# Loading the relation bases earlier, and making the one-hots of an edge sort in 16 bits for many columns at once

## The reference, cut to what matters

```
w = jnp.einsum('rb,bio->rio', att, basis)      # att (2, 30), basis (30, 512, 512), twice
...
msg = jnp.where((edge_type == 0)[:, None], msgs[0], msgs[1])
agg = jax.ops.segment_sum(msg, row, num_segments=x.shape[0])
```

## Time and profile before

| | us |
|---|---|
| median of 3 runs | 2412.63 (2412.43 to 2413.53) |
| profiled execution, its own time | 2412.91 |
| its span in the trace | 2411.2 |
| of that: up to the first sort matmul | 67.4 |
| sort | to 164 |
| counting | 170 to 365 |
| bias stage, up to the first attention work | to about 426 |

### The profile page before, as it was taken

The page is one execution under the profiler, slowest core; times in us unless marked ns, Lnnn a source line. Parts: engine busy times, 40 slices in busy tenths (PEclk is TensorE's granted clock), DMA queues, the critical chain, the costliest instruction groups (busy, mean ns, idle before and its releaser), DMA issues.

```text
span 2411.2 us, 36422 instructions
## 1 busy us (share of the span) xinstructions
PE 2207.0 (92%) x13669; PEld 1889.5 (78%) x13669; DVE 1628.0 (68%) x3598; ACT 1154.1 (48%) x1826; POOL 527.4 (22%) x398
## 2 busy tenths in 40 slices
PE   2788884899999999999999999999999999999999
PEld 0554443789988888998888999888899888877887
DVE  7789997548877646877754777765588775244234
ACT  3216668337773335775333777433477633322321
POOL 1200000016650003663000665100266400000000
PEclk9899996899999999999999999999999999999999
DMA  7978998211012202003101110320210231031023
GB/s 182 228 165 195 202 226 257 82 51 36 29 36 78 71 19 63 22 22 104 62 29 30 43 43 1 113 71 10 59 35 22 81 103 45 1 113 45 1 67 103
DMA packets 67363, 189.54 MB, mean 79 GB/s; under 512 B 6917, under 2 KB 7365, under 8 KB 66685
## 3 DMA queue, kind: packets, MB, share of 16 engines
q1 hardware_dynamic: 63498, 180.50, 27.8%
q10 hardware_dynamic: 3699, 6.76, 0.9%
HBM read 155.15 MB, written 32.07 MB: 78 GB/s over the span
## 4 chain that ended last, share of the span: by engine, by line
PE 70%; DVE 11%; issue 6%; ACT 6%; DVEq 3%; DMA 2%; SPq 1%; POOL 0%; ACTq 0%
PE PS L1032 10%; PE PS L1060 9%; PE PS L951 6%; PE PS L953 6%; PE PS L952 6%; PE PS L1046 6%; PE PS L937 5%; PE PS L941 4%; PE PS L938 4%; PE PS L1188 4%; PE PS L1198 4%; DVE chunk_hot L1652 2%; DVEq L1688 2%; DMA basis_t<-in_L_gnn_basis_dram 2%; ACT prob L1417 1%
## 5 line engine op out<-in xcount | busy, mean ns | idle before, releaser
L774 POOL TENSOR_SCALAR prob<-prob,inv_den 125x1000 f32<-125x1000 f32 x160 | 444.4, 2777 | 0.0
L1417 ACT ACTIVATE prob<-prob,neg_max 125x1254 f32<-125x1254 f32 x160 | 215.5, 1347 | 56.8 <-DVE neg_max L1908 56.7
L762 POOL TENSOR_TENSOR rstd<-var_eps,neg_half 125x2 f32<-125x2 f32 x45 | 33.4, 743 | 951.3 <-DVE var_eps L1578 951.3
L1903 DVE CUSTOM_DVE_ANT_0 prob<-PS,sbias 125x1254 f32<-125x1254 f32 x160 | 233.1, 1457 | 10.0 <-issue 7.3
L1060 PE MATMUL PS<-pT_hi,v_hi 125*128 125x250 f32 x800 | 236.1, 295 | 0.0
L1922 DVE TENSOR_TENSOR pT_lo<-PS,pT_hi 125x1000 fp32r<-125x1000 f32 x160 | 191.1, 1194 | 50.8 <-ACT pT_hi L1434 50.8
L1060 PE MATMUL PS<-pT_lo,v_hi 125*128 125x250 f32 x800 | 224.2, 280 | 0.0
L1060 PE MATMUL PS<-pT_hi,v_lo 125*128 125x250 f32 x800 | 222.5, 278 | 0.0
L1046 PE MATMUL PS<-ident,prob 125*125 125x125 f32 x1600 | 201.1, 273 | 5.6 <-DVE pT_lo L1925 5.5
L1046 PEld LDWEIGHTS PS<-ident,prob 125*125 125x125 f32 x1600 | 195.6, 188 | 12.5 <-issue 7.6
L1432 ACT ACTIVATE pT_hi<-PS 125x1000 fp32r<-125x1000 f32 x160 | 161.9, 1012 | 81.2 <-PE PS L1046 81.2
(11 more groups left out here) (327 smaller groups left out, 5728.3 us busy)
## 6 DMA issues: line engine op xcount, KB each, us to landing
basis_t<-in_L_gnn_basis_dram SPq DMA_DIRECT2D x32, 1920.0 KB, 13.1
sbias<-score_bias SPq DMA_DIRECT2D x40, 548.6 KB
adj<-adj SPq DMA_DIRECT2D x20, 546.9 KB
w_lo_raw<-in_L_gnn_m_w_dram SPq DMA_DIRECT2D x8, 1024.0 KB, 6.4
score_bias<-cnt SPq DMA_DIRECT2D x10, 548.6 KB
adj<-count_t SPq DMA_DIRECT2D x10, 546.9 KB
xc<-x_lat SPq DMA_DIRECT2D x12, 448.0 KB
x_first<-x_lat SPq DMA_DIRECT2D x10, 448.0 KB
```

Source lines behind the costliest of these rows:

```text
L774: pool.tensor_scalar(prob[u % 3][:, 0:SPLIT], prob[u % 3][:, 0:SPLIT], inv_den[0:T, u % 4:u % 4 + 1], None, ALU.mult)\
L1417: act.activation(prob[u % 3][:], prob[u % 3][:], ACT.Exp, bias=neg_max[0:T, u % 4:u % 4 + 1], accum_out=den[0:T, u % 4:u % 4 + 1]).then_in ...
L1903: v.tensor_tensor_reduce(prob[u % 3][:].rearrange("p (j s) -> p j s", j=3), PS[0:T, 0:3, 0:SB], sbias[p % 2][a][:].rearrange("p (j s) -> p ...
```

## The change

1. **Early loads.** SP issues 4 small broadcast loads (`att_rows`) and then basis loads 0 to 2, right behind the edges and ahead of the weights of the small network (`fw1` and others, 9 transfers counted by `fw_in`). The 16 tiny transfers into `att_z` are gone; POOL makes `att_z` from `att_rows` and a small mask `row_of` with 4 products.
2. **TensorE's order.** The wait for `fw_in`, the transpose and the first layer of the small network now stand ahead of all relation steps; then come 16 steps, and then the sort. ScalarE stores the first weights later for that.
3. **Sort.** SORT_BATCH is 16, so there are 10 batches (columns padded to 160). The edge values are kept in fp16. For a batch VectorE makes four tiles with one two-tensor instruction each: `chunk_hot` (196 by 16), `place_hot` (128 by 16), and `place_hot` times source and times target (`src_place`, `dst_place`). The 16 columns of a batch are innermost, so TensorE reads a column with a step of 32 bytes. It runs two fp16 matmuls for a column, one into bank 5 and one into bank 4, in place of one fp32 matmul.
4. **Behind the sort** three of the five unpacking instructions go.
5. **Counting.** `dst_hot` is made for two groups (four halves) by one two-tensor compare, in buffers that alternate by pair; the loop is written out for two pairs.
6. **Quads.** 16 in the sort (one or two behind each batch), 39 in counting (n % 5 in 1, 3), 5 in bias.
7. `slot_no` is an iota of 196 by 16 in place of 196.

```diff
-    SORT_BATCH = 8
+    SORT_BATCH = 16
...
-        STEPS_FIRST, STEPS_RANK = 2 * QL, 2 * QL
-        QUADS_SORT = [b for b in range(SORT_BATCHES) if b % 10 not in (0, 3, 6)]
-        QUADS_COUNT = [n for n in range(NG) if n % 8 in (1, 4, 7)]
+        STEPS_FIRST = 2 * QL
+        QUADS_SORT = [2 if b % 3 else 1 for b in range(SORT_BATCHES)]
+        QUADS_COUNT = [n for n in range(NG) if n % 5 in (1, 3)]
...
+            for l, att in enumerate((att1, att2)):
+                for r in range(R):
+                    sp.dma_start(att_rows[l][:, r:r + 1],
+                                 att[r, :].rearrange("(b a) -> b a", a=1).unsqueeze(1).to_broadcast([B, 4, 1]))\
+                        .then_inc(att_in, 16)
+            for n in range(3):
+                load_bases(n)
             sp.dma_start(fw1[:], f_w1).then_inc(fw_in, 16)
...
-            for n in range(NL):
+            for n in range(3, NL):
...
-            pool.iota(slot_no[:], [[1, TC]], base=0, channel_multiplier=0,
+            pool.iota(slot_no[:], [[1, TC], [0, SORT_BATCH]], base=0, channel_multiplier=0,
...
+                        pool.tensor_scalar(att_z[l][:, 24 + 4 * r:28 + 4 * r], row_of[:], att_rows[l][:, r:r + 1], None,
+                                           ALU.mult).then_inc(att_ready, 1)
...
-                    g = pe.matmul(PS[:, 5, 0:TC], place_hot[b % 2][:, i, :], chunk_hot[b % 2][:, i, :],
-                                  start=(c == 0), stop=(c == EC - 1))
+                    for bank, place in ((5, src_place), (4, dst_place)):
+                        g = pe.matmul(PS[:, bank, 0:TC], place[b % 2][:, :, i], chunk_hot[b % 2][:, :, i],
+                                      start=(c == 0), stop=(c == EC - 1))
...
+            v.wait_ge(x_sums, 2 * NT + 1)
             for b in range(SORT_BATCHES):
                 if b >= 2:
                     v.wait_ge(sort_used, b - 1)
...
+                v.tensor_tensor(chunk_hot[b % 2][:], by_slot(edge_chunk, TC), slot_no[:], ALU.is_equal)
+                if b:
+                    v.wait_ge(sort_hot, b)
+                v.tensor_tensor(place_hot[:], by_slot(edge_place, 128), slot_no[:, 0:128, :], ALU.is_equal)\
+                    .then_inc(place_done, 1)
+                v.wait_ge(place_done, b + 1)
+                v.tensor_tensor(src_place[b % 2][:], place_hot[:], by_slot(edge_src, 128), ALU.mult)
+                v.tensor_tensor(dst_place[b % 2][:], place_hot[:], by_slot(edge_dst, 128), ALU.mult).then_inc(sort_hot, 1)
...
+                if b == 0:
+                    v.tensor_tensor(dst_hot[turn][:], slot_no[:, 0:128, 0:4],
+                                    slot_dst[:, bass.ds(4 * it, 4)].unsqueeze(1).to_broadcast([128, 128, 4]), ALU.is_equal)
                 for h in range(2):
-                    v.tensor_scalar(dst_hot[b][:, h, :], node_no[:, 0:128],
```

More of the change, by code:

```diff
@@ L215, in gnn_kernel @@
         src_hot = [m(f"src_hot{i}", [128, 2, SW], bf16) for i in range(2)]
-        dst_hot = [m(f"dst_hot{i}", [128, 2, 128], bf16) for i in range(2)]
+        dst_hot = [m(f"dst_hot{i}", [128, 128, 4], bf16) for i in range(2)]
         count_add = [m(f"count_add{i}", [T, SW], i16) for i in range(2)]
@@ L231, in gnn_kernel @@
         m = Map(COUNT_END)
-        code, pos, pos_p, pos_c = (m(n, [128, EC]) for n in ("code", "pos", "pos_p", "pos_c"))
+        pos, pos_c = m("pos", [128, EC]), m("pos_c", [128, EC])
+        edge16 = m("edge16", [128, 4, ECP], f16)
+        edge_src, edge_dst, edge_place, edge_chunk = (edge16[:, i, :] for i in range(4))
         bucket_id = m("bucket_id", [128, NB])
@@ L241, in gnn_kernel @@
         base = m("base", [128, NB])
[L242 removed]
         PLACE_AT = m.at
[L244 to L245 removed]
+        src_place = [m(f"src_place{i}", [128, 128, SORT_BATCH], f16) for i in range(2)]
+        dst_place = [m(f"dst_place{i}", [128, 128, SORT_BATCH], f16) for i in range(2)]
+        chunk_hot = [m(f"chunk_hot{i}", [128, TC, SORT_BATCH], f16) for i in range(2)]
         node_no = m("node_no", [128, SW], f16)
@@ L271, in gnn_kernel @@
         att_z = [m(f"att_z{l}", [4 * B, 24 + 32]) for l in range(2)]
+        att_rows = [m(f"att_rows{l}", [4 * B, R]) for l in range(2)]
+        row_of = m("row_of", [4 * B, 4])
+        slot_no = m("slot_no", [128, TC, SORT_BATCH], f16)
+        slot_src = m("slot_src", [128, TC])
+        slot_dst = m("slot_dst", [128, TC], f16)
+        assert m.at <= TOP + 4 * 4 * D
         m = Map(COUNT_END)
@@ L1286, in steps_follow @@
                     steps_done[1] += 1
-            for b in range(13):
-                if b in QUADS_SORT:
-                    steps_follow(4)
+            for b in range(7):
+                steps_follow(4 * QUADS_SORT[b])
             act.wait_ge(z2_ps, 1)
@@ L1296, in _ @@
             z.then_inc(cond_hi, 1)
-            for b in range(13, SORT_BATCHES):
-                if b in QUADS_SORT:
-                    steps_follow(4)
+            for b in range(7, SORT_BATCHES):
+                steps_follow(4 * QUADS_SORT[b])
             for n in range(NG):
@@ L1695, in _ @@
             for b in range(2):
-                one_hot(0, b, True)
+                one_hot(0, b, 0, True)
             for b in range(2):
-                one_hot(1, b, False)
+                one_hot(1, b, 1)
                 add_group(0, b, b == 0)
-            with v.Fori(2, NG // 2) as it:
-                for b in range(2):
-                    one_hot(it, b, False)
-                    add_group(it - 1, b)
+            for b in range(2):
+                one_hot(2, b, 0)
+                add_group(1, b)
+            assert (NG // 2 - 3) % 2 == 0
+            with v.Fori(0, (NG // 2 - 3) // 2) as pair:
+                for turn in (1, 0):
+                    it = 2 * pair + (4 - turn)
+                    for b in range(2):
+                        one_hot(it, b, turn)
+                        add_group(it - 1, b)
             for b in range(2):
```

107 lines of the change are left out of this document (46 added, 61 removed).

## The result

The changed kernel takes 2450.55 us (median of 4 runs, 2444.58 to 2451.07), the kernel before 2412.62 on the same chip: a ratio of 1.015, with a 95% interval of 1.0135 to 1.0165. It is 38 us slower, where 2392.6 had been forecast. The profiled execution of it took 2444.58 us, 2442.8 of them in its span, 31.6 more than before. It is the quickest of the four; what is known of the 6 us between it and the other three is told at the end.

The account below looks back on a forecast made before the run. VectorE was taken to bound the kernel before, with DMA right behind; after the change, loads at 9.7 us each. 2412.9 - 22 (`csum` earlier) + 2 (bias) = 2392.9, median 0.3 lower: 2392.6 us, range 2376 to 2407.

Parts of the forecast that it names:

- sort on TensorE: Sort: 314 matmuls at 0.18 us each, 5.8 us a batch, 7.4 with quads, above VectorE's 5.2.
- the 136 of the loads: Sort: ten basis loads must be used by its end, which puts that end at about 136 us.
- 17 us for 16 quads: Sort: the quads' share of TensorE's time, added to its start at 56 us and the matmuls.
- the 32-byte step starves TensorE: Sort: matmuls cost s, `csum` at 260 + 314s, break-even 0.34 us; 2464 us at s = 0.5; chance 0.08.
- Start: Setup's beginning: basis loads 0 to 2 and `fw_in` land at about 44 us, sort matmuls start at 56.
- alone gain nothing: Start: earlier basis loads bring no gain, since load 3 lands at 64.6 us against 63.9 before.
- Sort on VectorE: Sort: two-tensor instructions at two elements per cycle, 5.2 us a batch, 52 us in all against 77; POOL's 10.5 us stop goes.
- The loads and counting: Sort and counting: dense basis loads, one each 9.7 us, set the pace; `csum` at 343 us against 365.2.
- the first rival: Counting: faster DMA leaves VectorE the pace, about 2373 us; chance 0.12 together with early TensorE.
- Bias: Behind counting: loads 30 and 31 come 10 to 20 us after its end, so 2 us are given back.
- Range and chances: Whole kernel: 2376 to 2407 us; faster 0.86, same 0.08, slower 0.06.

Follow-up runs that it names:

- step8: The changed kernel with its four sort tiles in groups of 4 columns, so TensorE steps 8 bytes and not 32: 2390.25 us.
- early_only: The kernel before with only the early loads, the new TensorE order and 18 quads in the sort for 14: 2408.18 us.
- early_fw: `early_only` with the nine small `fw_in` loads ahead of basis loads 0 to 2: 2393.08 us.
- best1: `step8` with the nine small `fw_in` loads ahead of basis loads 0 to 2 and `slot_no` 4 wide, not 16: 2379.51 us.
- place8: The changed kernel with only the weights `src_place` and `dst_place` at a step of 8 bytes, `chunk_hot` still at 32: 2451.21 us.
- step16: The changed kernel with all sort tiles at a step of 16 bytes: 2443.29 us.
- step32_fw: The changed kernel with only the nine small `fw_in` loads moved ahead of basis loads 0 to 2: 2442.59 us.
- best2: `best1` with `chunk_hot` at a step of 4 bytes: 2377.94 us.

## Why the prediction was wrong, point by point

- **The step that failed** is "sort on TensorE": "The operands are read with a step of 32 bytes, which no row shows, so neither end is sure. I take 0.18, the row of the same shape." It measured 0.36. The ends, 0.10 and 0.18, both came from contiguous rows; the range of the sum had no upper bound from the step, though the text named the step as unknown. What the runs show in its place: with each column in 16 bytes of its own the moving operand costs 1.84 ns a column, and the sort, not the loads, sets when counting begins. 314 x 0.18 = 56.5 us more.
- **The clock** was missing from it. The granted clock of the changed kernel, in windows:

```profile
55.00:60.00 5.00, 5.00 (x21) 1.91 (x14) 0.00 (x0) 4.94 (x5) 0.00 (x0) 1.00 0.84 189
60.00:67.00 7.00, 7.00 (x21) 2.72 (x19) 0.00 (x0) 6.57 (x11) 6.68 (x2) 0.53 0.97 212
67.00:200.00 133.00, 133.00 (x409) 45.83 (x408) 42.31 (x32) 8.29 (x14) 9.53 (x2) 0.56 0.59 141
```

  The matmuls are 0.36 us apart from 55.95 on, at clock 1.00, and still 0.36 (99.56 to 99.93) at the lower level. So the clock did not make them slow; it fell behind 60 us while they went on at the same spacing. What it costs is the other work between the sort's matmuls: the 15 quads before the last of them take 26.5 us, and at the upper level (1.06 for one, 1.92 for two in a row) would take 14.7; the second layer of the small network takes 4.3 and in `step8`, at the upper level, 2.3. Together 13.8 us.
- The sum closes: TensorE's own path in the forecast, 56 + 17 + 56.5 = 129.5 (it lay under the 136 of the loads), + 56.5 + 13.8 = 199.8; measured 200.5. Its 17 us for 16 quads stood by luck for 14.7 of quads and the 2.3 of the small network, which it had left out.
- **The rival "the 32-byte step starves TensorE"** had the mechanism, its break-even (0.34 us) and the sign, at a chance of 0.08. With s = 0.36 its formula gives `csum` at 373; 396.8 came. Of the 24 us 14 are the clock's, which the formula left out; the others lie behind the sort, 196 us from its end to `csum` where the formula has 187, since the loads hold counting at its end (VectorE waits 8.4 us at once there). What I held against the rival, that the fp32 record "already reads twice the bytes", was the wrong quantity: the table above goes by pieces of 16 bytes touched, 49 for the contiguous fp32 row, 196 here.
- **Start:** right, with two small misses that cancel: transpose at 45.9 (forecast 44), but the 16 steps took 5.2 us (7.3 forecast, at the lower clock), sort matmuls at 55.6 (56), the fourth basis load out at 54 us. That the early loads "alone gain nothing" is nearly so for this order: `early_only` is 4.9 us faster by the spans, 7.7 at `csum`. With the small loads first they bring 19 us (`early_fw`). I took the 9 transfers behind 5.9 MB as given, and did not price that order.
- **Sort on VectorE:** right, 1.79, 1.22, 1.23 and 1.22 us, 5.22 a batch (5.2). The `memset` of `count` no longer stops VectorE: `chunk_hot` at 67.33, in the midst of it, took 1.79 us:

```profile
60.32 2.85 POOL L759 TENSOR_TENSOR z<-z,z 16x1250 f32<-16x1250 f32 x1 [28.50 <-ACT z L1290]
63.12 10.57 POOL L773 MEMSET count<- 125x12540 f32 x1
```

  By the Trainium skill (SBUF — State Buffer, Who interferes with whom) only GpSimd instructions that read SBUF block a two-tensor instruction; the trace agrees. The other half shows in `best1`, where `src_place` at 43.6 took 3.74 us beside the multiplication `z`, which reads SBUF and itself took 5.23 us there.
- **The loads and counting:** the numbers are right where TensorE allows it, the mechanism by half. The kernel at 8 bytes, which has the forecast's 0.18 us, ended its sort at 139.5 (136), had `csum` at 338.5 (343) and took 2390.25 us (2392.6). In counting a pair of groups takes VectorE 3.6 us, as forecast. But a load does not take 9.7 us each: from 155.3 to 273.0 us SP issues 13 more of them, one each 9.05 us, VectorE's pace for five groups; VectorE is busy 100 of 100 us from 180 to 280, and the weight loads of counting wait 92 times for `src_hot`, 58.1 us in all, which the forecast had said they would no longer do. The loads stop VectorE once, for 11.0 us, behind the four other transfers that SP issues from 273.6 us on. That is the first rival ("VectorE paces counting") until 307 us and the forecast behind it, so the near hit of 343 is in part luck.
- **Bias:** nothing was given back (2 us forecast) between the two kernels: from `csum` to the end both profiled executions take the same to 0.1 us. In `step8` that part takes 5.8 us more, which eats the 4.5 us that its `csum` is early; the hit of 2390.25 on 2392.6 is luck to that extent.
- **Range and chances:** the range, up to 2407, had left the rival out.

## What to carry to other kernels

Before a tile is laid out for one engine, look at how the other reads it: a layout with the batch innermost makes VectorE's compare cheap and spreads TensorE's moving operand. Groups of 4 or 2 columns served both here. And where a price is unknown because of an address pattern, the bound has to come from that pattern, or the case against needs more than a few per cent. What TensorE waits for first, however small, belongs ahead of the large transfers in a queue: at `csum` that was worth 12 us here (`early_fw` against `early_only`) and 13 (`best1` against `step8`, with the narrower `slot_no`), but only 2 in the changed kernel, where TensorE's sort is the bound.

## What the runs showed of the hardware that was not expected

- TensorE's moving operand costs about 1.83 ns for each new 16 bytes, at either clock level (0.36 us for 196 columns at 1.00 and at 0.50 to 0.56); VectorE's reads of `slot_no` fit the same price. The weights at a step of 32 bytes show no cost beside matmuls 0.18 us apart.
- TensorE can be busy without a gap in the records, 133 of 133 us, and be granted 0.56 of its clock. "PE busy 100%" with a low clock is a sign to look at the spacing of the matmuls.
- SP is held at the issue of small transfers behind large ones. SP's timeline after the change, start and duration of the issue:

```profile
8.25 1.71 SPq L534 DMA_DIRECT2D basis_t<-in_L_gnn_basis_dram  x3
10.00 2.30 SPq L544 DMA_DIRECT2D fw<-in_L_gnn_f_w_dram  x1
12.34 6.98 SPq L545 DMA_DIRECT2D fw<-in_L_gnn_f_w_dram  x1
```

  In `best1`, ahead of the bases, each of these took 0.58 us.
- The runs of the changed kernel spread over 6.5 us (2444.6 to 2451.1). By the traces a difference of this size arises behind the setup, in code that no run changed. The profile of `place8` (2451.21 us) has `csum` at 396.83, as the changed kernel (2444.58) at 396.81, and then takes 2052.6 us to the end and not 2046.0. Its granted clock falls three more times there. The first, changed kernel and then `place8`:

```profile
570.00:590.00 20.00, 16.99 (x120) 16.00 (x119) 16.04 (x42) 14.46 (x25) 13.13 (x9) 1.00 0.11 28
570.00:590.00 20.00, 17.00 (x107) 15.92 (x106) 14.41 (x37) 13.01 (x23) 12.14 (x9) 0.91 0.19 55
```

  All 14 traces go by this: without such a fall the part from `csum` to the end takes 2045.7 to 2046.2 us (both kernels, `step16`, `step32_fw` and `early_fw`), with one 2048.8 (`early_only`), with three 2051.5 to 2053.4 (the other eight, `step8`, `best1` and `best2` among them). So a difference under some 7 us between two of these kernels is read from `csum` and not from the time. That the three other runs of the changed kernel had the falls fits their times, but they have no trace; what brings a fall about no run shows.
